# Router logits from separate products, routing three pairs behind, and register loads spread over eleven tiles

## The reference

```python
x = x + tanh(g_xattn) * xattn(layernorm(x), ctx, ctx, Wq, bq, ..., Wo, bo)   # scores are |q k| / 4
x = x + tanh(g_ffn) * ffn(layernorm(x), w_router, w1, b1, w2, b2)

def ffn(xf):                                   # xf: 4096 x 256
    probs = softmax(xf @ w_router)             # 8 experts
    topk_w, topk_idx = top_k(probs, 2)
    weights = sum(topk_w[..., None] * one_hot(topk_idx, 8), axis=1)
    h = gelu(einsum('te,ieh->tih', xf, w1) + b1)
    out = einsum('tih,ihe->tie', h, w2) + b2
    return sum(out * weights[..., None], axis=1)
```

## Time and profile before

| | |
|---|---|
| Median of 3 runs (lowest to highest) | 685.94 us (685.66 to 686.71) |
| The profiled execution's own time | 687.67 us |
| Its span, first to last instruction | 685.9 us |
| Mean granted clock of TensorE, as a share of full speed | 0.986 |
| PE busy | 655.3 us, 96% of the span |
| DVE, ACT, POOL busy | 69%, 50%, 44% |
| Stages of the span | setup to 20, attention to 254, transition to 326, full tiles to 553, small tiles and end to 686 |

### The profile page before, as it was taken

How to read it: one execution, slowest core, us unless ns; L and a number is a source line. 1 busy time by engine, 2 the same in 40 slices (tenths; PEclk the granted TensorE clock), 3 DMA queues, 4 the chain that set the end, 5 groups by cost and what they waited for, 6 DMA issues and landing times.

```text
span 685.9 us, 21479 instructions
## 1 busy us (share of the span) xinstructions
PE 655.3 (96%) x6779; PEld 578.2 (84%) x6780; DVE 473.9 (69%) x1328; ACT 342.7 (50%) x771; POOL 303.3 (44%) x420
## 2 busy tenths in 40 slices
PE   8899999999999998899999999999999899999993
PEld 6799999999999888798889898998778788888882
DVE  5667887888887866778657565565554547777773
ACT  4668767777777665432424233332323325454541
POOL 7323476676777454761523233232322323333332
PEclk9989999999999999999999999999999999999997
DMA  5234355545544446236333232333321223333322
GB/s 198 65 107 143 125 160 167 171 141 161 167 156 138 146 139 181 80 89 174 36 62 48 47 46 48 46 55 55 48 49 33 40 49 56 50 50 55 52 32 23
DMA packets 51325, 63.25 MB, mean 92 GB/s; under 512 B 4577, under 2 KB 46951, under 8 KB 51111
## 3 DMA queue, kind: packets, MB, share of 16 engines
q1 hardware_dynamic: 37695, 43.94, 21.4%
q0 software_dynamic: 13440, 18.14, 15.7%
q10 hardware_dynamic: 104, 0.04, 0.0%
HBM read 37.39 MB, written 24.63 MB: 90 GB/s over the span
## 4 chain that ended last, share of the span: by engine, by line
PE 47%; DVE 5%; issue 4%; POOL 3%; DMA 1%; DVEq 1%; POOLq 0%; ACT 0%; ACTq 0%
PE banks L1713 16%; PE banks L1691 14%; PE banks L1730 8%; PE banks L1752 7%; POOL routed L802 2%; PE banks L1703 1%; DMA out_dram<-prob_t,meta 1%; DVE prob L1241 1%; POOL l_exp L785 1%; DVEq L624 1%; PE banks L1742 1%; DVE prob_t L1259 1%; DVE v_area L1243 1%; DVE prob_t L1263 0%; DVE xn_t L1248 0%
## 5 line engine op out<-in xcount | busy, mean ns | idle before, releaser
L945 ACT ACTIVATE stage<-banks,bias_t 128x256 f32<-128x256 f32 x200 | 83.8, 470 | 176.3 <-PE banks L1691 175.3
L1691 PE MATMUL banks<-xn_t,w_hi 128*128 128x256 f16 x800 | 133.1, 273 | 3.7 <-issue 1.9
L1713 PE MATMUL banks<-w,prob 128*128 x800 | 132.6, 273 | 3.1 <-DVE v_area L1243 2.3
L839 POOL DMA_INDIRECT out_dram<-prob_t,meta x46 | 72.7, 1580 | 128.7 <-DVE prob_t L1263 113.0
L1691 PE MATMUL banks<-xn_t,w_lo 128*128 128x256 f16 x400 | 109.0, 273 | 0.0
L1713 PE MATMUL banks<-w,v_area 128*128 x400 | 109.0, 273 | 0.0
L1691 PEld LDWEIGHTS banks<-xn_t,w_hi 128*128 x800 | 77.2, 98 | 15.3 <-issue 6.3
L1713 PEld LDWEIGHTS banks<-w,prob 128*128 128x128 f16 x800 | 78.2, 98 | 13.5 <-issue 4.4
L960 ACT ACTIVATE stage<-banks,bias_t 128x128 f32<-128x128 f32 x168 | 52.7, 363 | 66.8 <-PE banks L1730 66.0
L802 POOL DMA_INDIRECT routed<-row,pos x64 | 69.8, 1091 | 27.9 <-issue 14.6
L1622 PEld LDWEIGHTS banks<-v_area,prob_t 128*128 128x128 f32 x640 | 74.9, 194 | 5.4 <-issue 1.2
(11 more groups left out here) (250 smaller groups left out, 1324.0 us busy)
## 6 DMA issues: line engine op xcount, KB each, us to landing
stage<-in_L_ffn_w_dram SPq DMA_DIRECT2D x32, 512.0 KB, 4.8
x_row<-routed SPq DMA_DIRECT2D x25, 265.0 KB
x_in<-in_x_dram SPq DMA_DIRECT2D x16, 256.0 KB, 3.9
x_res<-in_x_dram SPq DMA_DIRECT2D x16, 256.0 KB
out_dram<-x_res SPq DMA_DIRECT2D x16, 256.0 KB, 2.8
x_row<-routed SPq DMA_DIRECT2D x21, 132.5 KB, 2.2
routed<-pad_rows SPq DMA_DIRECT2D x9, 265.0 KB
out_dram<-prob_t,meta POOLq DMA_INDIRECT x67, 3.8
```

Of the source, the lines that this page charges most:

```text
L839: pool.indirect_dma_start(out[:, :], bass.IndirectOffsetOnAxis(ap=meta_of(j, pj)[:, b, E:E + 1].bitcast(U32), axis=0), y[:, pj, b], None, ...
L945: ins = act.activation(hid[:, c], H[:, q, c % PER * SLOTS:(c % PER + 1) * SLOTS], ACT.Gelu_apprx_tanh, bias=k.bias_t[:, bass.ds(e * HC + c ...
L1691: mm = pe.matmul(H[:, q, c % PER * SLOTS:(c % PER + 1) * SLOTS], w[:, bass.ds(e, 1), i, c * P:(c + 1) * P].rearrange("p a n -> p (a n)"), ...
L1713: mm = pe.matmul(Y[pj][:, b * D:(b + 1) * D], h[:, pj, c, b * P:(b + 1) * P], w[:, bass.ds(e, 1), c, :].rearrange("p a n -> p (a n)"), sta ...
```

## The change

With v = x + tanh(g) (attention Wo + bo), the logits are (v - mean) / spread times W. The mean is taken out of W once, in the setup: PE sums its columns with a stationary operand of -0.5, and DVE adds 2/256 of that to W (`centred`). Then v W splits in parts: x W is the normalised query row, already turned for the query projection, times W (`row_parts`, PE) and multiplied by its own spread (`keep_part`, DVE; `spread_of`, POOL); the attention part is the turned attention times Wo W (`router_product`, once, PE; its 8 columns stand behind Wo's 256 in `wo_t`, so that `project_attention` makes 264 columns); bo W is a constant (`base`). The division by the spread comes after the choice of the two best (`shift_logits`, DVE), as it doesn't change their order.

The row's transposes, the copy of the turned rows and the product after them are gone. `ranks`, `choose`, `place_rows` and `scatter_rows` work on pair j - 3 instead of j - 4 in step j, and the hand-written sequence after the last pair is put in a new order. The loop now covers tiles 8 to 13, and tiles 14 to 24 are straight code; each reads two small tiles' numbers, on PE one after the second quarter of the first layer and one between the halves of the second layer. DVE finishes tile 2 behind the hidden rows of tile 4. The wait of tile 24's second layer is split into four.

```diff
-FACTOR_OPS = (3, 4)
+FACTOR_OPS = (4, 4)
+HEAD_FACTORS = 3
+PAIRS_KEPT = 4
...
+                dve.wait_ge(column_sums, 1)
+                for c in range(KC):
+                    dve.scalar_tensor_tensor(k.w_router[:, c], banks[:, XT[0], 0:E], 2.0 / D, k.w_router[:, c],
+                                             ALU.mult, ALU.add).then_inc(centred, 1)
...
+                pe.wait_ge(ld_wr, 16)
+                pe.wait_ge(made, 11)
+                for c in range(KC):
+                    mm = pe.matmul(banks[:, XT[0], 0:E], k.minus_half[:].to_broadcast([P, P]), k.w_router[:, c],
+                                   start=(c == 0), stop=(c == KC - 1))
+                mm.then_inc(column_sums, 1)
                 turn_weight(2, WV)
                 pe.wait_ge(key_lo_sb, 1)
                 turn_weight(3, WO)
+                pe.wait_ge(centred, KC)
+                for c in range(KC):
+                    mm = pe.matmul(banks[:, XT[0], E:2 * E],
+                                   k.bias_t[:, n_bias + 3 * KC + c:n_bias + 3 * KC + c + 1].to_broadcast([P, P]),
+                                   k.w_router[:, c], start=(c == 0), stop=(c == KC - 1))
+                mm.then_inc(base_ps, 1)
...
-LOOP_TILES = range(8, FULL_TILES - 5 - (FULL_TILES - 5) % 2)
+PRELOAD_TILES = -(-SMALL_TILES // 2)
+LOOP_TILES = range(8, FULL_TILES - PRELOAD_TILES - (FULL_TILES - PRELOAD_TILES) % 2)
...
                             pool.tensor_scalar(x_norm[:, tile], x_in[:, j % 2, tile], neg_mean[:, 0, tile, 0:1],
                                                rstd[:, 0, tile, 0:1], ALU.add, ALU.mult).then_inc(norm1, 1)
+                        ready(pool, part_sb, j, 2)
+                        pool.tensor_tensor(k.spread_of[:, j % 2], var_eps[:, 0], rstd[:, 0], ALU.mult)\
+                            .then_inc(factors1, 1)
 
                 def odd(j):
-                    if exists(j - 4):
-                        scatter_rows(j - 4)
+                    if exists(j - 3):
+                        scatter_rows(j - 3)
...
                 even(PAIRS + 1)
-                scatter_rows(PAIRS - 4)
                 even(PAIRS + 2)
                 scatter_rows(PAIRS - 3)
...
-                def copy_rows(j):
-                    ready(act, x2t_ps, j)
-                    ready(act, logit_ps, j - 1)
-                    act.activation(x2_t[:].rearrange("p c n -> p (c n)"), TURN, ACT.Copy).then_inc(x2t_sb, 1)
+                def copy_product():
+                    act.wait_ge(product_ps, 1)
+                    act.activation(k.wo_t[:, :, D:D + E], ROUTE[:, 0:KC * E].rearrange("p (c e) -> p c e", c=KC), ACT.Copy)\
+                        .then_inc(product_sb, 1)
...
+                def keep_part(j):
+
+                    ready(dve, part_ps, max(j, HEAD_PAIRS - 1))
+                    ready(dve, factors1, j, FACTOR_OPS[0])
+                    at = j % 2 * 2 * E
+                    for tile in range(2):
+                        dve.scalar_tensor_tensor(kept[:, j % PAIRS_KEPT, tile], NORM[:, at + tile * E:at + (tile + 1) * E],
+                                                 k.spread_of[:, j % 2, tile, 0:1], k.base[:], ALU.mult, ALU.add)\
+                            .then_inc(part_sb, 1)
+
+                def shift_logits(j):
+
+                    ready(dve, router, j, ROUTER_OPS, 3)
+                    ready(dve, factors2, j, FACTOR_OPS[1], 3)
+                    for tile in range(2):
+                        dve.tensor_scalar(l_shift[:, tile], best[:, tile], best[:, tile, 0:1], rstd[:, 1, tile, 0:1],
+                                          ALU.subtract, ALU.mult).then_inc(shift_sb, 1)
...
                     if part == 1:
-                        dve.tensor_copy(logits[:].rearrange("p t e -> p (t e)"), ROUTE[:, 0:2 * E]).then_inc(router, 1)
+                        dve.scalar_tensor_tensor(logits[:], k.banks[:, 0:2, D:D + E], k.gates[:, 0:1],
+                                                 kept[:, j % PAIRS_KEPT], ALU.mult, ALU.add).then_inc(router, 1)
...
-                        place_rows(j - 4)
+                        place_rows(j - 3)
+                        shift_logits(j - 3)
...
                     if follows(j + 1):
+                        keep_part(j + 1)
                         low_queries(j + 1, PROJ)
...
                 finish_rows(1, 0, 1)
+                for q in range(HID_BANKS):
+                    split_hidden(4, 0, q)
+                low_rows(5)
                 finish_rows(2, 1, 0)
-                tile_pipeline(dve, step, 4)
+                finish_rows(3, 1, 1)
+                tile_pipeline(dve, step, 5)
...
                     for tile in range(2):
                         for c in range(KC):
-                            mm = pe.matmul(PROJ[:, tile * D:(tile + 1) * D], attn_t[:, c, tile * P:(tile + 1) * P],
+                            mm = pe.matmul(k.banks[:, tile, 0:D + E], attn_t[:, c, tile * P:(tile + 1) * P],
                                            k.wo_t[:, c], start=(c == 0), stop=(c == KC - 1))
                     mm.then_inc(wo_ps, 1)
 
-                def turn_rows(j):
-                    ready(pe, norm2, j, 2)
-                    ready(pe, ot_sb, min(j + 1, PAIRS - 1), KC)
-                    turn_pair(TURN, row[:, j % ROWS_HELD, :, 0:D], x2t_ps)
-
-                def router_logits(j):
-                    ready(pe, x2t_sb, j)
-                    ready(pe, places, j - 1, PLACE_OPS, 1)
+                def row_parts(j, rows):
+
+                    at = j % 2 * 2 * E
                     for tile in range(2):
                         for c in range(KC):
-                            mm = pe.matmul(ROUTE[:, tile * E:(tile + 1) * E], x2_t[:, c, tile * P:(tile + 1) * P],
+                            mm = pe.matmul(NORM[:, at + tile * E:at + (tile + 1) * E], rows[:, c, tile * P:(tile + 1) * P],
                                            k.w_router[:, c], start=(c == 0), stop=(c == KC - 1))
-                    mm.then_inc(logit_ps, 1)
+                    mm.then_inc(part_ps, 1)
...
                         for q in range(HID_BANKS):
                             first_layer(j, e, q)
-                            small_experts(pe, experts, j, q, HID_BANKS)
+                            if q == 1:
+                                small_experts(pe, experts, j, 0, 2)
...
                             second_layer(j, e, pj, b)
+                            if b == 0 and isinstance(j, int):
+                                small_experts(pe, experts, j + 1, 1, 2)
...
-                    if exists(j - 4):
-                        ranks(j - 4)
+                    if exists(j - 3):
+                        ranks(j - 3)
+                    if j == 0:
+                        row_parts(0, xn_t)
+                        row_parts(1, k.xn_t_1)
                     if follows(j + 1):
                         ready(pe, xt_sb, j + 1)
+                        row_parts(j + 1, xn_t)
...
-                    if exists(j - 3):
-                        turn_rows(j - 3)
+                    if j == 1:
+                        router_product()
                     if exists(j - 2):
                         project_attention(j - 2)
-                    if exists(j - 3):
-                        router_logits(j - 3)
```

195 lines of the change are left out of this document (104 added, 91 removed).

## The result

The changed kernel takes 689.47 us (median of 12 runs, 686.85 to 692.39), the kernel before, run beside it, 684.56 (12 runs, 682.32 to 686.71). The ratio is 1.0072, with an interval of 1.0053 to 1.0092: slower, where 676.6 and faster had been forecast. The profiled execution took 688.41 us around a span of 686.6, against 687.67 around 685.9 before.

The account below looks back on a forecast made before the run. The prediction took PE's own work to bound attention and most full tiles, with waits on POOL and DVE chains in the transition. Terms -1.2 - 3.9 - 4.2 = -9.3 us, off the 685.94 median, gave 676.6 us, range 674.5 to 679.

Parts of the forecast that it names:

- the full 0.40: Attention, steady state: PE's work per pair falls by 0.40 us, from 15.00 to 14.60, and all of it counts.
- these thin covers: Attention: slack of DVE, ACT and POOL before PE waits, such as 0.6 us before the next scores and 3.4 for `shift_logits`.
- The pair's own work: Attention: 14.60 us on PE per pair, with `row_parts` costing 0.81 us in each even half step.
- The rest of attention: Attention terms: -16.4 us removed, +11.3 for `row_parts`, +0.8 for the wider projection, +1.2 for saving lost in `odd(14)`.
- The rival of DVE as the bound: Attention: DVE, waiting on POOL at `shift_logits`, bounds the pair; slower, 690 us at 1 us of stall; chance 0.07.
- The head: Start: products for column sums and `base`, 0.81 us ahead of the value products, cost +0.3 us (between 0 and 0.8).
- The transition: Last pairs to first full tiles: -2.8 us from the earlier chain and -1.1 from tile 5; sum -3.9, from -5 to 0.
- Its mechanism: Transition: a scatter group moves into `odd(15)`, so POOL's chain from `norm_factors` starts 2.5 us earlier; -2.8 on `ranks(15)`.
- the 281 to 282 and 3: Transition, sign of being right: `ranks(15)` near 281 to 282 us, with an idle time of about 3 before it.
- Rival 1: Transition: PE's idle time lowers the clock; a fall costs 3.4 us, giving 680.0; chance 0.22.
- The wait for tile 5's low half: Transition: PE's 1.13 us wait for DVE goes, as `finish_rows(2)` moves behind tile 5's rows; -1.1 us.
- The expert tiles: Straight steps: reads spread at four per step leave 0.5 us each; -4.2 us, from -8.8 to -0.5.

Follow-up runs that it names:

- e5: Kernel before, with eight unread eight-column products added between the ranks and the query product of each even half step, 14 times: 711.49 us, ratio 1.0392.
- e1: Changed kernel with row_parts of pair j + 1 moved behind the query product in the even half step: 672.42 us, ratio 0.9841 to the kernel before.
- e3: Changed kernel with row_parts behind the query product and bo loaded and transposed apart: 672.09 us, ratio 0.9835 to the kernel before.
- e11: Kernel before, with eight eight-column products added behind the query product, into another bank: 697.96 us, ratio 1.0100.
- e14: Changed kernel with row_parts behind the query product, run again in another group: 674.36 us, ratio 0.9851 to the kernel before.
- e17: Changed kernel with row_parts behind the query product, run again without idle products: 673.42 us, ratio 0.9847 to the kernel before.
- e6: Changed kernel with eight idle products of 128 columns added between the ranks and row_parts: 689.23 us, ratio 1.0055 to the kernel before.
- e10: Changed kernel with row_parts behind the query product, run again beside the changed kernel: 684.81 us, ratio 0.9905 to the kernel before.
- e2: Changed kernel with bo given rows, a load and a transpose of its own: 687.92 us, ratio 1.0063 to the kernel before.
- e4: Kernel before, with the full-tile loop ending at 14 instead of 20 and the small tiles' reads in two places: 675.57 us, ratio 0.9878.
- e15: Kernel before, with only the shorter loop and spread reads, run again in another group: 675.55 us, ratio 0.9868.
- group 4: Four kernels on one chip beside the kernel before (690.63 us): changed, row_parts behind, narrow products behind, row_parts behind with old reads; 693.36, 684.81, 697.96, 691.90 us.
- e12: Changed kernel with row_parts behind the query product and the old loop and reads, run again: 691.90 us, ratio 1.0027 to the kernel before.
- e16: Changed kernel with row_parts behind the query product and 30 idle products in the first even half step, run again: 672.60 us, ratio 0.9836.
- e7: Changed kernel with row_parts behind the query product and the old loop and places of the reads: 690.39 us, ratio 1.0058 to the kernel before.

## Why the prediction was wrong, point by point

**The step that failed** is the one on the pair: "So I take the full 0.40, bounded below by zero if one of these thin covers fails." I asked which other engine could bound the pair and took PE's own time as the sum of its durations. I had the clock as a rival only for the transition, behind waits. But `row_parts` moved eight narrow products from the odd half step to directly behind values and the ranks in the even one, and there PE loses its clock without waiting at all. Seven falls of 1.7 us are 11.9, against the 11.75 that attention grew. That the two agree so closely is partly chance: the first six half steps grew by 2.75 us, and the steady pairs, 0.29 shorter each without a fall, gave that back. e5 makes these falls in the kernel before with nothing but such products; e1, e3, e11, e14 and e17 show that they don't come with the query product in between, as long as PE has no wait there. So the cause is shown as far as the place goes. What it is in these products that lets the clock go isn't: e6 left half of the falls.

**The pair's own work** was sized nearly right: 7.85 + 6.86 = 14.71 without a fall, against 14.60. `row_parts` costs 0.89, not 0.81. The rest of attention came as forecast: from scores(0) to scores(31) e1 needs 222.81 us against 223.55, 0.7 less, where the terms of this stretch gave 0.2.

**The rival of DVE as the bound** said slower and, for 1 us of stall a pair, 690 us. That 689.47 was measured is chance: in the changed kernel's own profile PE waits nowhere in attention's steady part. An engine without cover there is, but it is ACT (e10), in kernels whose pair takes 14.66 us, and only on two of the five chips of the experiments.

**The head**: +0.3 was forecast, +3.95 came. I counted the products and not the fifth load, behind which the transpose of all biases waits. In that execution the clock fell in the wait. e2 and e3 show that this isn't what makes the kernel slower: without it the falls stand elsewhere in the first half steps. In the twelve other profiles with this head scores(0) begin at 20.46 to 22.24 us, in the five with the old one at 20.36 to 22.31, 21.0 in the mean of either. So the late start belongs to this execution, and the term of +0.3 isn't refuted; the spread is only wider than my range.

**The transition** gave more than forecast. From scores(31) to tile 6's transposes my terms were -3.9 and, for `odd(15)`, -1.26; measured were -6.8. A part of that may be a fall that the kernel before has at 246.8 us, behind scores(31), and the changed one hasn't: e4 and e15, with the old order and without this fall, need 86.5 and 86.7 us for the stage against 87.3. Against them the new order gains 6.0 to 6.2, where 5.2 was forecast. `ranks(15)` came 37.0 us behind scores(31), before 42.5. Its mechanism held with one addition: DVE's mask of pair 14 waited 2.30 us, because POOL, which reads the mask of pair 13, now does so only behind `norm_factors(15)`:

```profile
285.23 0.19 DVE L1185 TENSOR_TENSOR mask<-expert_no,best_f 128x32 f32<-128x32 f32 x1 [2.30 <-POOL row L830]
```

With the falls of attention out of the way (e1, e14, e17) `ranks(15)` started at 280.5 to 280.8 us behind waits of 1.7 to 3.3, near the 281 to 282 and 3 that I had named. Rival 1, a fall in the transition, did come (287.5 to 291 us), but cost little here: PE waited 1.65 us for the choice of pair 15 behind it. Where it came behind `ranks(15)`, in e14, it cost the 2.8 us shown above. The wait for tile 5's low half is gone, as said.

**The expert tiles**: forecast -4.2, measured -8.1 in the profile and 8.0 and 8.2 in e4 and e15. The term was mis-sized: that each read takes 0.5 us of PE's sequencer once the queue is past its lead doesn't hold for four reads spread over a step. They cost nothing; six, of which four stand at the quarters of the first layer, do. I had also written that the spacing doesn't matter for the sum; no run here separates it from the number. (5.5 less 0.8 is 4.7, not 4.6, which changes nothing.) The total is the one that I had put beside the Trainium skill ("DMA: Bandwidth & Descriptors", "Latency and other measured facts"), but not by its price: one read still holds 0.304 us of the queue here, not 600 ns.

**With the falls out of the way the total was nearly right, but by luck.** e1, e14 and e17 are 11.2, 9.4 and 10.6 us faster than the kernel before; the forecast was 9.3. But 8.0 to 8.2 of that are the reads, for which I had 4.2. What the whole new router adds to them is 3.2 us by e1 and e4, whose intervals overlap, and 1.2 by e14 and e15, where my terms gave 5.1; on the chip of group 4 it adds nothing (e12). The simplest version, the kernel before with the reads spread, has nearly the whole gain. Part of what attention and the transition gain is lost again behind them: the stage from tile 6 to the first small product takes 214.3 us in e1 and 212.9 in e4, and in e1 PE waits 0.81 us for tile 8's rows in it. The Trainium skill ("TensorE: Matmul & The Clock Gate", Part 1) says that the throttled clock is the default and that activity lifts it, and warns of idle gaps. The falls of the head agree with the warning: the clock fell in a wait of 2.71 us. Those of attention don't: they came in an engine that was busy for 180.00 of 180 us, so no gap is needed.

## What to carry to other kernels

When narrow products are added to a dense TensorE, look at what stands around them, and read the granted clock over the stage, not only the idle times. Here it was enough to put the query product (256 columns, 1.97 us) between them and the narrow ones ahead; 0.44 us of products of 128 columns were not. A saving on the bounding engine uses up the slack of all the others, so list who is next and how late one stall of that engine would make it. Loads of single numbers cost nothing here at four per step of 10.92 us, and 1.5 us at six. Measure a change's parts apart: here one small part, the reads, had most of the gain.

## What the runs showed of the hardware

- TensorE's granted clock fell from 1.00 to 0.50 within a row of products with 34, 128 and 8 columns that had no idle time in it (values 2.25 us, ranks, `row_parts` 0.9), for 3.4 us each time, in about every second even half step; with the query product of 256 columns between the ranks and `row_parts` it never did from 60 to 240 us where PE had no wait just ahead of the scores or the values (e1, e3, e14, e16, e17).
- A fall that is removed can come back at the next such place: e2 and e16 moved falls of the first 48 us and gained 1 us at most by it.
- ACT stands still for 0.7 to 1.5 us in the middle of its copies on two of the five chips of the experiments (11 times from 60 to 250 us in e10, 9 in e7) and hardly on the others (twice in e1). The same kernel took 672.42, 674.36 and 673.42 us on three chips and 684.81 on a fourth, where the kernel before lost only 5.5 to 7 us. The cause is open.
- A TensorE read of one number from SBUF into a register holds the queue for 0.304 us (median, straight steps) and was hidden wholly at four reads per step of 10.92 us.
